# A fused attention and expert kernel: the long product with V behind the third exp scores, the laying of the maxima and block 0's product behind the sixth, the max units of a group in another order

## The chip, the cores and the metric

One core of one Trainium2 chip. The metric is the device time of one execution in microseconds (us); lower is better.

## What is computed

The input `x` is (2, 512, 128): two batches b of 512 tokens with 128 channels. The part that this change touches is causal attention with 16 heads of 8 channels: q, k and v come from modulated and rotated projections of `x`, and

```
scores = einsum('bhsd,bhtd->bhst', q, k) / sqrt(8)      # causal mask, softmax over t
out    = einsum('bhst,bhtd->bhsd', softmax(scores), v)
x      = x + out @ w_out.T
```

After it come a mixture of 2 shared and 8 routed experts, and a layer that applies the best 3 of 8 zones to each batch. All of it is float32 in the reference.

## The kernel before

**Tiling.** The 2 batches x 16 heads are taken as 8 groups n = 0 to 7 of 4 heads (`GROUPS`, `HG`). A softmax needs the row maxima ahead of the exp, so each group is scored twice. The *max scores* have queries on partitions: TensorE writes a *unit* (`scores_for_max`, L1407, and for the diagonal unit L1402) into one of three PSUM banks (`RING_BANKS`), and VectorE adds the mask and reduces it (`reduce_max`, L772). For groups 2 to 7 a group has 11 units, in this text P (two pieces of 256 columns, 2 of them), T (384 columns, 4 of them), F (512 columns, 4 of them) and D (block 0 of all four heads, 4 pieces of 128, one). Groups 0 and 1 have 12 of another cut. A unit can be written only when the unit three before it has been reduced (`wait_ring`).

**The maxima.** When all units of a group are reduced, GpSimd puts the maxima into a padded tile (`place_max`, L644 and L646), TensorE *lays* them (`lay_max_under_q`, L1420, 4 small matmuls into the unused bank of the sixth scores' slot), and ScalarE copies them under the queries (`copy_qm`, L1109).

**The exp scores.** They have keys on partitions, six products E0 to E5 per group (`scores_for_exp`: E0 to E3 at L1443, E4 at L1447, E5 at L1452) into two PSUM slots in turn: E(u) waits for the exp of E(u-2). E0 also waits for `copy_qm` of its group. ScalarE takes the exp of each (`exp`, L1105). GpSimd zeroes the triangles of a tile when two exps are done (`affine_select`, L672: c = 0, 1, 2) and, behind the last, spreads the last queries (L658), which the next E5 needs.

**The product with V.** `weigh_v` (L1467) has two parts: *block 0's product* `weigh_v(n, 0, 0, S)` (8 instructions, needs the triangle c = 0 and that the sums before are copied out) and the *long product*, key blocks 1 to 3 (24 instructions, needs all triangles). ScalarE copies the sums out of PSUM (`copy_pv`, L1115), and SyncE stores them.

**Order.** Everything is written out by hand. TensorE does a *pass* for each group n, and inside it interleaves E0 to E5 of group n, the long product of group n-1, the max units that `max_units(n, i)` hands out in 11 slices i (`maximum(i)`), the laying of group n+1 and block 0's product of group n. `LEAD` says how many units of group n+2 are done in pass n (7; `FIRST` is 4 for group 1). Before the change a pass from 2 to 5 is, for TensorE:

```
E0 F E1 F F | long product n-1 | D E2 E3 P P T E4 | block 0 of n | T | lay n+1 | T E5 T F
```

ScalarE's pass is exp 0, exp 1, `copy_pv(n-1)`, exp 2, a weight cast (`split_high`, L1200, where `SPLITS` has (n, 0)), exp 3, exp 4, `copy_qm(n+1)`, exp 5, a second cast (where it has (n, 2)). There are seven casts: (3,0) (3,2) (4,0) (4,2) (5,0) (5,2) (6,0). GpSimd's pass is triangle 0; wait for exp 3; `place_max(n+1)`; triangle 1; `split_low` (L618); wait for exp 5; triangle 2; spread last queries; `split_low`.

**SyncE's queue** goes in order. Its pass n issues for group n+3 `load_k` (L455), `pad_q` (L433, 4 transfers, waits until group n+1's units are written), `pad_k` (L446), `load_q` (L461), then `store_sums(n)` (L466, waits for `copy_pv(n)`) and the weight loads of `EXPERT_LOADS[n]` (L474, waited for by `split_high`). Around them stand `gather(0)` in pass 3 (L483 and L488, waits until the sums of groups 0 to 3 are stored) and in pass 4 `store_inverse(0)` (L496, waits for `invert(0)`, L791, which VectorE does behind unit 8 of group 6) and `spread_inverse(0)` (L504). The last weight load, k = 6, stands behind `store_sums(4)`.

Of the kernel before, what the change touches and what calls it, by code (L numbers as in the profile page):

```python
# [14 lines left out]
P = 128  # L15
B, S, D = 2, 512, 128
NT = B * S
H, HD = 16, 8
HG = 4
NG = H // HG  # L20
GROUPS = B * NG
# [12 lines left out]


SPREAD_UNITS = [[(j, qb, i * 2 * P) for i, qb in enumerate(blocks)] for blocks in ((0, 1), (2,), (3,)) for j in range(HG)]
PAIRED_UNITS = [[(2 * h2 + i, 1, i * 2 * P) for i in range(2)] for h2 in range(2)]
PAIRED_UNITS += [[(j, qb, 0)] for qb in (2, 3) for j in range(HG)] + [[(j, 0, j * P) for j in range(HG)]]
MX_UNITS = [SPREAD_UNITS if n < 2 else PAIRED_UNITS for n in range(GROUPS)]
MX_LIST = [(n, u) for n in range(GROUPS) for u in range(len(MX_UNITS[n]))]  # L40
RING_BANKS = (0, 1, 7)

# [9 lines left out]
N_UNITS = len(UNITS)  # L52


LEAD, FIRST = 7, 4
BY_PE = 1
SPILLS = 2
SLICES = 11
# [5 lines left out]
def units_to(n, u=0):  # L64

    return sum(len(x) for x in MX_UNITS[:n]) + u

# [6 lines left out]

RING_ORDER = [("max", 0, _u) for _u in range(len(MX_UNITS[0]))]
RING_ORDER += [("max", 1, _u) for _u in range(2)] + [("lay", 0)] + [("max", 1, _u) for _u in range(2, FIRST)]
# [70 lines left out]
def program(nc, io, scratch, out):  # L147
# [9 lines left out]
    with ctx:  # L157
# [255 lines left out]
        def _(sp):  # L413
# [12 lines left out]
            def pad_q(n):  # L426

                s = n % 2
                if n >= 2:
                    sp.wait_ge(mx_full, units_to(n - 1) if n < 4 else units_to(n - 1) - 1)  # L430
                for j in range(HG):
                    q = head_rows(j)
                    sp.dma_start(f32_of(q_pad[s][q, j, :]), laid(n, 0)[q, :]).then_inc(q_padded[s], 16)  # L433
# [157 lines left out]
        def _(pool):  # L591
# [72 lines left out]
            for n in range(GROUPS):  # L664
                for c in range(3):

                    pool.wait_ge(exp_done, STU * n + 2 * c + 2)
                    if c == 1 and n + 1 < GROUPS:
                        place_max(n + 1)
                    for o in ((0,) if c < 2 else (0, 2 * P)):  # L670
                        tri = probs[n % 2][:, c, :, o:o + P]
                        last = G.affine_select(out=tri, in_=tri, compare_op=ALU.is_ge, fill=0.0, base=0,  # L672
                                               pattern=[[0, HG], [1, P]], channel_multiplier=-1)
                    last.then_inc(masked, 1)
                    if c == 2 and n + 1 < GROUPS:
                        spread_last_queries(n + 1)
                    if n == 0 and c == 0:
                        turn(1)
                    if n == 0 and c == 1:
                        spread_last_queries(0)  # L680
                        turned(1)
                    if n == 0 and c:

                        pool.wait_ge(hi_ready, 4 + c)
                        pool.wait_ge(rep_ready, 2 * BY_PE + 2)
                        for written in spilled:
                            pool.wait_ge(written, 16 * SPILLS)
                        G.tensor_tensor(qk_lo[:, c - 1, :], roped[:, c - 1, :], f32_of(qk_hi[:, c - 1, :]),
                                        ALU.subtract).then_inc(lo_ready, 1)
                    if c and (n, 2 * c - 2) in SPLITS:  # L690
                        split_low(SPLITS[n, 2 * c - 2])
# [37 lines left out]
        def _(dve):  # L729
# [34 lines left out]
            def reduce_max(n, u):  # L764
# [3 lines left out]
                dve.wait_ge(mx_full, units_to(n, u + 1))  # L768
                for j, qb, o in MX_UNITS[n][u]:
                    width = P * (qb + 1)  # L770
# [252 lines left out]
        def _(act):  # L1023
# [63 lines left out]
            def exp(n, u):  # L1087
                s = n % 2
                c, h2 = divmod(u, 2)
                act.wait_ge(st_full, STU * n + u + 1)  # L1090
                if n >= 2 and u == 0:
                    act.wait_ge(pv_full, n - 1)
                if n == 1 and u == 4:
                    act.wait_ge(roped_ready, 6)
                at_ = slot_of("exp", n, u)
                if c < 2:
                    w = S - c * P
                    o, scores = probs[s][:, c, 2 * h2:2 * h2 + 2, 0:w], ST[:, at_:at_ + 2, 0:w]
                elif h2 == 0:
                    o = probs[s][:, 2, :, 0:2 * P]  # L1100
                    scores = ST[:, at_:at_ + 2, :].rearrange("p b (j q) -> p (b j) q", j=2)
                else:
                    o = probs[s][:, 2, :, 2 * P:3 * P]
                    scores = ST[:, at_, :].rearrange("p (j q) -> p j q", j=HG)
                A.activation(o, scores, ACT.Exp, scale=float(1.0 / np.sqrt(np.float32(HD)))).then_inc(exp_done, 1)  # L1105
# [5 lines left out]
            def copy_pv(n):  # L1111
                act.wait_ge(pv_full, n + 1)
                if n >= 2:
                    act.wait_ge(stored[n % 2], 16 * (n // 2))
                A.copy(o_sb[n % 2][:], PV).then_inc(pv_copied, 1)  # L1115
# [77 lines left out]
            def split_high(k):  # L1193

                hi, lo, c, at_ = chunks[k]
                act.wait_ge(ld_raw[k], 16)
                if k == UP_COLS // S:
                    for written in spilled:
                        act.wait_ge(written, 2 * 16 * SPILLS)
                A.copy(hi[:, c:c + S], raw[:, at_:at_ + S]).then_inc(w_hi, 1)  # L1200
# [25 lines left out]
            for n in range(GROUPS):  # L1226
                exp(n, 0)
                if n == 1:
                    take_hi(1)
                exp(n, 1)  # L1230
                if 0 < n < GROUPS - 1:
                    copy_pv(n - 1)
                exp(n, 2)
                if n == 0:
                    copy_v(1)
                if (n, 0) in SPLITS:
                    split_high(SPLITS[n, 0])
                exp(n, 3)
                exp(n, 4)
                if n == 0:  # L1240
                    take_hi(0)
                if n + 1 < GROUPS:
                    copy_qm(n + 1)
                if n == GROUPS - 1:
                    exp_of_minus_logits(0)
                exp(n, 5)
                if (n, 2) in SPLITS:
                    split_high(SPLITS[n, 2])
# [30 lines left out]
        def _(pe):  # L1279
# [103 lines left out]
            def scores_for_max(n, u):  # L1383
                s = n % 2
                pieces = MX_UNITS[n][u]
                if n == 0:
# [111 lines left out]
            def project_out(b):  # L1498
                pe.wait_ge(onorm_ready, b + 1)
                pe.wait_ge(ld_small, 16)  # L1500
                if b == 0:
                    wait_ring("out", 0)
                    T.matmul(ring("out", 0), small[:, W_OUT:W_OUT + D], packed_out[:],
                             start=True, stop=True).then_inc(proj_ready, 1)
                else:
                    pe.wait_ge(last_norm, 1)
                    T.matmul(MISC, small[0:EARLY, W_OUT:W_OUT + D], packed_out[0:EARLY, :], start=True, stop=False)
                    T.matmul(MISC, small[:, W_LAST:W_LAST + D], o_sb[1][:], start=False,
                             stop=True).then_inc(proj_ready, 1)
# [123 lines left out]
                T.matmul(MISC[:, 80:80 + TOPZ], ones_row[:], zw[:, b, :], start=True, stop=True).then_inc(z_bc, 1)  # L1633


            for n in range(GROUPS):

                def maximum(i):
                    for unit in max_units(n, i):
                        scores_for_max(*unit)  # L1640

                scores_for_exp(n, 0)
                maximum(0)
                scores_for_exp(n, 1)
                maximum(1)
                maximum(2)
                if n:
                    weigh_v(n - 1, 1, P, S)
                    weigh_v(n - 1, 2, 2 * P, S)
                    weigh_v(n - 1, 3, 3 * P, S)  # L1650
                maximum(3)
                scores_for_exp(n, 2)
                if n == GROUPS - 1:
                    project_out(0)
                scores_for_exp(n, 3)
                maximum(4)
                maximum(5)
                maximum(6)
                scores_for_exp(n, 4)
                if n == GROUPS - 1:  # L1660
                    route_experts(0)
                weigh_v(n, 0, 0, S)
                maximum(7)
                if n + 1 < GROUPS:
                    lay_max_under_q(n + 1)
                maximum(8)
                scores_for_exp(n, 5)
                maximum(9)
                maximum(10)
            up(0)  # L1670
            weigh_v(GROUPS - 1, 1, P, S)
            weigh_v(GROUPS - 1, 2, 2 * P, S)
# [107 lines left out]
```

## Time and profile before

| | us |
|---|---|
| median of 3 runs (lowest, highest) | 180.97 (180.79, 181.07) |
| the profiled execution, whole | 180.98 |
| its span, first to last instruction | 179.1 |
| attention passes 1 to 7 | from 34.0 to about 90 |

Times of rows are us from the span's start. In a row, "x24" is the number of instructions merged, and a bracket at the end is the idle time of the engine ahead of it and what ended it. PE is TensorE (PEld its weight loads), DVE VectorE, ACT ScalarE, POOL GpSimd, SPq SyncE's DMA queue. Matmuls are pipelined: the distance between two starts tells what one costs the engine, not its duration.

### The profile page before, as it was taken

The page shows a single profiled execution, that of the slowest core. Times are in us where ns is not written, and L with a number is a line of the kernel's source. Part 1 is how long each engine was busy: PE and PEld are TensorE (multiplying, and loading weights), DVE is VectorE, ACT ScalarE, POOL GpSimd, SP SyncE. Part 2 cuts the span into 40 slices and gives each one's busy share as a digit, 9 for nine tenths or more (in the row PEclk, how much of TensorE's full clock was granted, in tenths as well). Part 3 has the DMA queues.
Part 4 walks back from the last instruction along what each step waited for, and adds up shares of the span by engine and source line. Part 5 has one row for each costly group of instructions (what it writes and reads, how often), then busy time and mean ns, then how long its engine had stood idle before and what let it go on. Part 6 is the DMA issues. An engine that isn't in the chain of part 4 may idle for free.

```text
span 179.1 us, 3278 instructions
## 1 busy us (share of the span) xinstructions
PE 168.9 (94%) x943; PEld 116.8 (65%) x944; DVE 138.9 (78%) x444; ACT 134.3 (75%) x224; POOL 93.8 (52%) x117
## 2 busy tenths in 40 slices
PE   6899999899999999988999999996999989999992
PEld 2656575565666666653758767864687867788881
DVE  5588989989898899980586999699799658637551
ACT  3569177688768888889734787953879999999970
POOL 5508088985463969688532522021769931676000
PEclk9999999999999999999999999999999999999999
DMA  4824775676686567520110899960760000001001
GB/s 144 294 46 107 191 203 159 218 234 213 166 267 208 143 194 194 164 94 5 62 51 17 231 345 344 347 178 4 241 230 0 0 4 0 0 2 59 0 4 59
DMA packets 15349, 24.28 MB, mean 136 GB/s; under 512 B 2844, under 2 KB 4828, under 8 KB 15308
## 3 DMA queue, kind: packets, MB, share of 16 engines
q1 hardware_dynamic: 14532, 23.29, 42.2%
q10 hardware_dynamic: 800, 0.79, 1.7%
q8 instruction: 8, 0.13, 0.3%
q14 instruction: 9, 0.07, 0.1%
HBM read 18.71 MB, written 5.27 MB: 134 GB/s over the span
## 4 chain that ended last, share of the span: by engine, by line
PE 70%; DVE 11%; ACT 7%; issue 6%; POOL 4%; DVEq 0%; ACTq 0%; POOLq 0%
PE psum L1407 11%; PE psum L1540 10%; PE psum L1541 9%; PE psum L1542 9%; PE psum L1467 8%; PE psum L1443 7%; PE psum L1286 3%; PE psum L1338 2%; PE psum L1352 2%; ACT t_probs L1105 2%; DVE psum L772 2%; DVE t_raw L924 1%; PE psum L1402 1%; ACT t_q_pad L1155 1%; PE psum L1447 1%
## 5 line engine op out<-in xcount | busy, mean ns | idle before, releaser
L772 DVE CUSTOM_DVE_ANT_0 psum<-psum,t_causal 128x128 f32<-128x128 f32 (+3 forms) x128 | 58.6, 525 | 5.8 <-PE psum L1407 3.0
L1105 ACT ACTIVATE t_probs<-psum 128x1024 f32<-128x1024 f32 (+2 forms) x48 | 40.9, 883 | 8.2 <-PE psum L1443 5.2
L1407 PE MATMUL psum<-t_stacked,t_q_pad 96*128 96x256 f32 (+2 forms) x104 | 33.3, 391 | 0.5 <-DVE t_row_max L772 0.2
L1407 PEld LDWEIGHTS psum<-t_stacked,t_q_pad 96*128 96x128 f32 x104 | 18.4, 189 | 12.4 <-DVE t_row_max L772 10.2
L672 POOL TENSOR_SCALAR_AFFINE_SELECT t_probs<-t_probs 128x512 f32<-128x512 f32 x32 | 20.5, 651 | 9.0 <-ACT t_probs L1105 9.0
L944 DVE SCALAR_TENSOR_TENSOR t_q_pad<-psum,t_zw_all,t_q_pad 128x512 fp32r<-128x512 f32 x24 | 17.8, 748 | 9.3 <-ACT t_q_pad L1153 9.2
L1139 ACT ACTIVATE psum<-psum 128x512 f32<-128x512 f32 x40 | 23.4, 586 | 0.9 <-PE psum L1542 0.3
L703 POOL TENSOR_TENSOR t_q_pad<-t_raw,t_q_pad 128x512 fp32r<-128x512 f32 x8 | 10.8, 1357 | 21.0 <-ACT t_q_pad L1155 21.0
L1467 PE MATMUL psum<-t_probs,t_v_all 128*32 128x512 f32 (+3 forms) x256 | 20.6, 439 | 0.0
L772 DVE DVE_READ_ACCUMULATOR2_ANT t_row_max<- 128x1 f32 x128 | 18.0, 141 | 0.0
L1153 ACT ACTIVATE t_q_pad<-psum,t_zw_all 128x512 fp32r<-128x512 f32 x24 | 16.5, 688 | 1.2 <-PE psum L1542 0.6
L1443 PE MATMUL psum<-t_q_two,t_k_pad 104*128 104x512 f32 (+1 forms) x48 | 13.5, 380 | 0.4 <-ACT t_q_two L1109 0.4
L1540 PE MATMUL psum<-t_stacked,t_up_hi 128*128 128x512 f32 x32 | 13.8, 430 | 0.0
L1541 PE MATMUL psum<-t_stacked,t_up_lo 128*128 128x512 f32 x32 | 12.6, 394 | 0.0
L1542 PE MATMUL psum<-t_stacked,t_up_hi 128*128 128x512 f32 x32 | 12.6, 393 | 0.0
L947 DVE TENSOR_TENSOR t_q_pad<-psum,t_q_pad 128x512 fp32r<-128x512 f32 x16 | 10.9, 680 | 1.7 <-ACT t_q_pad L1155 1.3
L931 DVE TENSOR_TENSOR psum<-psum,t_stacked 128x512 f32<-128x512 f32 x16 | 11.0, 690 | 1.4 <-DVE t_top L852 0.7
L1467 PEld LDWEIGHTS psum<-t_probs,t_v_all 128*32 128x32 f32 x256 | 6.5, 109 | 7.8 <-issue 2.9
L1155 ACT CAST t_q_pad<-psum 128x512 fp32r<-128x512 f32 x16 | 9.4, 588 | 1.2 <-DVE psum L931 1.0
L1540 PE MATMUL psum<-t_q_pad,t_dn_hi 128*128 128x512 f32 x24 | 9.8, 408 | 0.4 <-POOL t_q_pad L703 0.2
L1443 PEld LDWEIGHTS psum<-t_q_two,t_k_pad 104*128 104x128 f32 x48 | 8.4, 189 | 2.5 <-issue 0.9
L1541 PE MATMUL psum<-t_q_pad,t_dn_lo 128*128 128x512 f32 x24 | 9.5, 396 | 0.0
(233 smaller groups left out, 369.6 us busy)
## 6 DMA issues: line engine op xcount, KB each, us to landing
t_stacked<-scratch SPq DMA_DIRECT2D x16, 256.0 KB, 5.7
t_probs<-in_L_ffn_Wa SPq DMA_DIRECT2D x2, 1024.0 KB, 11.5
scratch<-t_o_sb SPq DMA_DIRECT2D x7, 256.0 KB, 2.1
t_raw<-in_experts SPq DMA_DIRECT2D x7, 256.0 KB, 3.6
t_stacked<-scratch SPq DMA_DIRECT2D x9, 192.0 KB, 3.7
t_q_pad<-scratch SPq DMA_DIRECT2D x28, 48.0 KB
scratch<-t_dn_hi SPq DMA_DIRECT2D x2, 512.0 KB, 3.4
t_q_two<-scratch SPq DMA_DIRECT2D x5, 192.0 KB, 2.6
```

Of the source, the lines that this page charges most:

```text
L672: last = G.affine_select(out=tri, in_=tri, compare_op=ALU.is_ge, fill=0.0, base=0, pattern=[[0, HG], [1, P]], channel_multiplier=-1)
L772: last = V.tensor_tensor_reduce(scores, scores, causal[:, S - width:S], 1.0, 3 * BIG, ALU.add, ALU.max, row_max[s][:, qb, j:j + 1])
L944: V.scalar_tensor_tensor(h_lo[i % SLOTS], hidden_of(i), weight_of(i), f32_of(h_hi[i % SLOTS]), ALU.mult, ALU.subtract).then_inc(lo_done, 1)
L1105: A.activation(o, scores, ACT.Exp, scale=float(1.0 / np.sqrt(np.float32(HD)))).then_inc(exp_done, 1)
L1139: A.activation(o, pair_of(i)[:, 0, :], func, scale=scale).then_inc(act_done, 1)
L1153: A.activation(h_hi[i % SLOTS], hidden_of(i), ACT.Identity, scale=weight_of(i)).then_inc(hi_done, 1)
L1407: last = T.matmul(bank[:, o:o + width], q_pad[s][0:TOP, j, qb * P:(qb + 1) * P], stacked[0:TOP, n, 0:width], start=True, stop=True)
L1443: last = T.matmul(ST[:, at_ + i, 0:S - c * P], k, q[:, c * P:S], start=True, stop=True)
L1467: last = T.matmul(PV[32 * j:32 * j + 32, lo:hi], v_all[:, v0:v0 + 32], probs[n % 2][:, c, j, o:o + hi - lo], start=(kb == 0 and lo == 0), ...
L1540: T.matmul(o, hi, x_hi, start=start, stop=False)
L1541: T.matmul(o, lo, x_hi, start=False, stop=False)
L1542: return T.matmul(o, hi, x_lo, start=False, stop=stop)
```

## The change

TensorE's pass, `LEAD` and the order of a group's units change, with two calls that move on ScalarE and GpSimd. From 2 to 5, TensorE's pass is now

```
E0 T T E1 D T E2 F | long product n-1 | F E3 P E4 P F E5 | lay n+1 | F | block 0 of n | T
```

In passes 0 and 1 the units are those of the old order (pass 0: E0 T T E1 T T E2 F F F E3 F E4 P P E5, lay, T, block 0, T T). `LEAD` is 5, so that pass 0 does two units less and pass 6 two more. In pass 7, which has no units, the order stays. `pad_q` for groups 5 to 7 waits for one unit more, since the last unit of a group now reads the padded queries.

```diff
-PAIRED_UNITS = [[(2 * h2 + i, 1, i * 2 * P) for i in range(2)] for h2 in range(2)]
-PAIRED_UNITS += [[(j, qb, 0)] for qb in (2, 3) for j in range(HG)] + [[(j, 0, j * P) for j in range(HG)]]
-MX_UNITS = [SPREAD_UNITS if n < 2 else PAIRED_UNITS for n in range(GROUPS)]
+HEAD_PAIRS = [[(2 * h2 + i, 1, i * 2 * P) for i in range(2)] for h2 in range(2)]
+THREE, FOUR = [[[(j, qb, 0)] for j in range(HG)] for qb in (2, 3)]
+DIAGONAL = [[(j, 0, j * P) for j in range(HG)]]
+PAIRED_UNITS = HEAD_PAIRS + THREE + FOUR + DIAGONAL
+TURNED_UNITS = HEAD_PAIRS + FOUR[0:2] + THREE[0:3] + DIAGONAL + THREE[3:4] + FOUR[2:4]
+MX_UNITS = [SPREAD_UNITS if n < 2 else PAIRED_UNITS if n == 2 else TURNED_UNITS for n in range(GROUPS)]
...
-LEAD, FIRST = 7, 4
+LEAD, FIRST = 5, 4
...
-                    sp.wait_ge(mx_full, units_to(n - 1) if n < 4 else units_to(n - 1) - 1)
+                    sp.wait_ge(mx_full, units_to(n - 1) - (n == 4))
...
+                    if c == 1 and 2 <= n < GROUPS - 1:
+                        place_max(n + 1)
                     pool.wait_ge(exp_done, STU * n + 2 * c + 2)
-                    if c == 1 and n + 1 < GROUPS:
+                    if c == 1 and n < 2:
                         place_max(n + 1)
...
                 exp(n, 1)
-                if 0 < n < GROUPS - 1:
-                    copy_pv(n - 1)
                 exp(n, 2)
                 if n == 0:
                     copy_v(1)
                 if (n, 0) in SPLITS:
                     split_high(SPLITS[n, 0])
+                if 0 < n < GROUPS - 1:
+                    copy_pv(n - 1)
                 exp(n, 3)
...
+            for n in range(GROUPS - 1):
...
                 scores_for_exp(n, 0)
                 maximum(0)
-                scores_for_exp(n, 1)
                 maximum(1)
+                scores_for_exp(n, 1)
                 maximum(2)
+                maximum(3)
+                scores_for_exp(n, 2)
+                maximum(4)
                 if n:
                     weigh_v(n - 1, 1, P, S)
                     weigh_v(n - 1, 2, 2 * P, S)
                     weigh_v(n - 1, 3, 3 * P, S)
-                maximum(3)
-                scores_for_exp(n, 2)
...
+                maximum(5)
                 scores_for_exp(n, 3)
-                maximum(4)
-                maximum(5)
                 maximum(6)
                 scores_for_exp(n, 4)
...
-                weigh_v(n, 0, 0, S)
                 maximum(7)
-                if n + 1 < GROUPS:
-                    lay_max_under_q(n + 1)
                 maximum(8)
                 scores_for_exp(n, 5)
+                lay_max_under_q(n + 1)
                 maximum(9)
+                weigh_v(n, 0, 0, S)
                 maximum(10)
```

## Rows read from the trace of the kernel before

**Rows 1.** The page: busy time by engine

```profile
PE 168.9 (94%) x943; PEld 116.8 (65%) x944; DVE 138.9 (78%) x444; ACT 134.3 (75%) x224; POOL 93.8 (52%) x117
```

**Rows 2.** Stretches from E0 to E0, passes 0, 3, 6: busy PE, PEld, DVE, ACT, POOL; clock

```profile
24.57:34.04 9.47, 8.54 (x45) 5.23 (x43) 8.97 (x39) 6.83 (x12) 8.37 (x11) 1.00 0.59 174
...
50.52:58.75 8.23, 8.21 (x64) 5.27 (x64) 7.46 (x35) 6.66 (x10) 4.78 (x8) 1.00 0.75 227
...
75.21:83.03 7.82, 6.80 (x54) 3.69 (x53) 5.15 (x23) 6.90 (x11) 5.90 (x10) 1.00 0.28 94
```

**Rows 3.** The order of time, TensorE, pass 3 (E0 at 50.52)

```profile
50.52 0.63 PE L1443 MATMUL psum<-t_q_two,t_k_pad 104*128 104x512 f32 x2
...
51.68 0.67 PE L1407 MATMUL psum<-t_stacked,t_q_pad 96*128 96x512 f32 x2
52.29 1.50 PE L1467 MATMUL psum<-t_probs,t_v_all 128*32 128x384 f32 x24
53.72 0.50 PE L1402 MATMUL psum<-t_k_pad,t_q_two 96*128 96x512 f32 x1
54.06 0.87 PE L1443 MATMUL psum<-t_q_two,t_k_pad 104*128 104x384 f32 x4
54.77 1.09 PE L1407 MATMUL psum<-t_stacked,t_q_pad 96*128 96x256 f32 x5
55.70 0.63 PE L1447 MATMUL psum<-t_q_two,t_k_pad 104*128 104x256 f32 x4
56.26 1.06 PE L1467 MATMUL psum<-t_probs,t_v_all 128*32 128x512 f32 x8
57.25 0.44 PE L1407 MATMUL psum<-t_stacked,t_q_pad 96*128 96x384 f32 x1
57.53 0.40 PE L1420 MATMUL psum<-t_minus_ident_b,t_max_pad 128*128 128x128 bf16 x4
```

**Rows 4.** The order of time, VectorE, pass 3: around the two products

```profile
52.96 0.73 DVE L772 CUSTOM_DVE_ANT_0 psum<-psum,t_causal 128x512 f32<-128x512 f32 x1
53.61 0.14 DVE L772 DVE_READ_ACCUMULATOR2_ANT t_row_max<- 128x1 f32 x1
54.26 0.30 DVE L772 CUSTOM_DVE_ANT_0 psum<-psum,t_causal 128x128 f32<-128x128 f32 x1 [0.51 <-PE psum L1402]
...
57.73 0.57 DVE L772 CUSTOM_DVE_ANT_0 psum<-psum,t_causal 128x384 f32<-128x384 f32 x1 [0.26 <-PE psum L1407]
```

**Rows 5.** The order of time, end of pass 0 (E5 is L1452)

```profile
30.21 1.06 PE L1467 MATMUL psum<-t_probs,t_v_all 128*32 128x512 f32 x8
...
32.87 0.47 PE L1452 MATMUL psum<-t_stacked 104*128 104x512 f32 x1 [0.51 <-POOL t_stacked L658]
```

**Rows 6.** The order of time, ScalarE, passes 4 and 6

```profile
62.09 0.59 ACT L1115 COPY t_o_sb<-psum 128x512 f32<-128x512 f32 x1 [0.58 <-PE psum L1467]
...
80.01 0.61 ACT L1200 CAST t_dn_hi<-t_raw 128x512 fp32r<-128x512 f32 x1
80.52 1.73 ACT L1105 ACTIVATE t_probs<-psum 128x768 f32<-128x768 f32 x2
...
82.40 0.58 ACT L1109 CAST t_q_two<-psum 8x512 fp32r<-8x512 f32 x1 [0.15 <-PE psum L1420]
```

**Rows 7.** SyncE's queue, 62.7 to 74.4 us

```profile
62.70 0.34 SPq L466 DMA_DIRECT2D scratch<-t_o_sb  x1
...
70.40 0.42 SPq L496 DMA_DIRECT2D scratch<-t_sums  x1
...
73.95 0.43 SPq L474 DMA_DIRECT2D t_raw<-in_experts  x1
```

**Rows 8.** DMA issues of 73.9 to 74.5 us: count, KB, us to landing

```profile
t_raw<-in_experts SPq DMA_DIRECT2D x1, 256.0 KB, 4.4
```

**Rows 9.** TensorE: warm-up matmuls, and its longest silence later on

```profile
1.39 3.36 PE L1286 MATMUL psum<-t_warm 128*128 128x512 bf16 x8 [1.39 <-POOL t_warm L593]
...
122.64 0.28 PE L1614 MATMUL psum<-t_ident_r,t_gate 128*32 128x128 f32 x1 [1.62 <-DVE t_gate L878]
```

More of the change, by code:

```diff
@@ L1633, in zone_spread @@
                 T.matmul(MISC[:, 80:80 + TOPZ], ones_row[:], zw[:, b, :], start=True, stop=True).then_inc(z_bc, 1)
-            for n in range(GROUPS):
+            for n in range(GROUPS - 1):
                 def maximum(i):
@@ L1643, in _ @@
                 maximum(0)
+                maximum(1)
                 scores_for_exp(n, 1)
-                maximum(1)
                 maximum(2)
+                maximum(3)
+                scores_for_exp(n, 2)
+                maximum(4)
                 if n:
@@ L1650, in _ @@
                     weigh_v(n - 1, 3, 3 * P, S)
-                maximum(3)
-                scores_for_exp(n, 2)
-                if n == GROUPS - 1:
-                    project_out(0)
+                maximum(5)
                 scores_for_exp(n, 3)
-                maximum(4)
-                maximum(5)
                 maximum(6)
                 scores_for_exp(n, 4)
-                if n == GROUPS - 1:
-                    route_experts(0)
-                weigh_v(n, 0, 0, S)
                 maximum(7)
-                if n + 1 < GROUPS:
-                    lay_max_under_q(n + 1)
                 maximum(8)
                 scores_for_exp(n, 5)
+                lay_max_under_q(n + 1)
                 maximum(9)
+                weigh_v(n, 0, 0, S)
                 maximum(10)
+            last = GROUPS - 1
+            scores_for_exp(last, 0)
+            scores_for_exp(last, 1)
+            weigh_v(last - 1, 1, P, S)
+            weigh_v(last - 1, 2, 2 * P, S)
+            weigh_v(last - 1, 3, 3 * P, S)
+            scores_for_exp(last, 2)
+            project_out(0)
+            scores_for_exp(last, 3)
+            scores_for_exp(last, 4)
+            route_experts(0)
+            weigh_v(last, 0, 0, S)
+            scores_for_exp(last, 5)
             up(0)
```

## The prediction

> **What bounds the kernel now.** I read the page first: TensorE is busy 94%, VectorE 78% and ScalarE 75% [rows 1]. Busy time says little of a pipelined engine, so next the stretches from one E0 to the next. Pass 3 takes 8.23 us, and passes 1 to 5 are alike; in it VectorE is busy 7.46 us, ScalarE 6.66, and the granted clock is full, 2.4 GHz [rows 2]. No engine is full by itself. The order of time shows why: TensorE and VectorE take turns. During the long product TensorE writes no unit for 1.43 us (52.29 to 53.72), during block 0's product none for 0.99 us [rows 3], and VectorE, which has three banks in hand at most, runs dry behind both: 0.51 and 0.26 us [rows 4]. TensorE then waits for a bank elsewhere.
>
> How much can come back? TensorE's own cost of a pass is the sum of distances between starts: E0 or E1 0.47 us (51.68 is two of these and one F of 0.23 behind 50.52), E2 and E3 together 0.71, long product 1.43, E4 with the turn to the next product 0.56, block 0's product 0.99, and a T behind a product 0.28 (57.25 to 57.53) [rows 3]. With a plain T at 0.18, P at 0.23, E5 at 0.24 and the laying at 0.21 (estimates by columns from F), it comes to some 7.6 us. VectorE needs 7.46 less what it pays for running dry. So 0.6 us a pass is the ceiling, and TensorE sets it.
>
> **The change, part by part.** Each removes and adds no arithmetic; only places move.
>
> *A pass from 2 to 5.* I walk TensorE from E0 = 0: E0, T, T, E1, D to 1.53. The second T behind D needs the bank of the first T: written 0.47, read by VectorE 0.48 later (57.25 to 57.73 [rows 3, 4]), reduced some 0.63 after that with the read-out (F takes 0.65 + 0.14 from 52.96 to the end of 53.61's row, a T in proportion): 1.63, so 0.1 us of wait. T and E2 to 2.16, F to 2.39, the turn 0.1 and the long product 1.43: 3.92, call it 3.95. Then F 0.34 (the first matmul behind a product costs what D does, 53.72 to 54.06 [rows 3]), E3 0.35, P 0.23, E4 0.47, P 0.23, F 0.23, E5 0.24: the laying begins at 6.04; laying 0.21, F 0.23, turn and block 0's product 1.09, T 0.28: **7.85 us**, against 8.23. VectorE still runs dry at the long product, by about 0.35 us, but no longer at block 0's: F, F and the rest of a P are in hand, some 1.9 us for a hole of 1.7. That gap costs nothing as long as TensorE is the fuller engine.
>
> *Covers.* The laying waits for `place_max`: the last F is reduced at 3.95 + 0.54 + 0.79 = 5.28, placing and its signals are put at 0.65 more (an estimate: two small GpSimd operations, each between 0.2 and the 0.58 of the shortest ScalarE row [rows 6]): 5.93, just ahead of 6.04. `place_max` no longer waits for exp 3; that matters in pass 6, below, and in the others the laying was not late. ScalarE: the long product ends later, so `copy_pv` begins at 4.1 rather than 3.3, but behind exp 2 and the cast it no longer waits 0.58 us [rows 6]. Then exp 3, exp 4, `copy_qm` end at about 7.1; the next E0 wants it at 7.85. exp 5 now stands behind a later laying; triangle 2 has the time to the next long product, 4 us, to hide.
>
> *Pass 1* keeps the old order of units for group 2: D (some 1.05 us of VectorE, by its four pieces) is last, and `place_max(2)` waits for exp 3: the laying is 0.3 later. 8.15 us.
>
> *Pass 0.* E5 is started at 32.87 by GpSimd's spreading of the last queries (L658), whose chain the change does not touch [rows 5]. Block 0's product stood ahead of it at 30.21, in TensorE's idle time. Now the laying, T, block 0's product and two T come behind: 0.30 + 0.21 + 0.28 + 1.09 + 0.35, so E0 of pass 1 is at **35.1 instead of 34.04** [rows 2]: 1.06 us lost. The two units fewer of `LEAD` 5 give nothing here, since pass 0 waits for GpSimd; they are done in pass 6, where VectorE was busy 5.15 of 7.82 us [rows 2], beside other work.
>
> *Sum so far.* E0 of pass 4 = 35.1 + 8.15 + 2 x 7.85 = 58.95 (before: 58.75), of pass 5 66.8, of pass 6 some 74.65, with 0.2 for the padded queries of group 7, whose loads move later with the queue: 74.85 (before: 75.21). Pass 6, free of waits, would take 7.35, since its laying no longer waits for exp 3: E0 of pass 7 at 82.2 against 83.03.
>
> *SyncE's queue.* This is the cover that fails. `copy_pv(3)` began at 62.09 [rows 6], and its store went at 62.70 [rows 7]; now it begins at 58.95 + 4.1 = 63.05, **0.96 later**. Everything behind it is a chain: the gather waits until the store landed, then the loads of group 7, `store_inverse` at 70.40, its landing, `spread_inverse`, `store_sums(4)`, and the last weight load at 73.95 [rows 7], landed 4.4 us later [rows 8], at 78.35. `invert(0)` ends at 70.9, before the queue wants it at 71.4. So the load lands at 79.3. Its cast stood behind `copy_pv` at 80.01 [rows 6] and had 1.7 us to spare. Now it would begin at 74.85 + 3.35 = 78.2, ahead of `copy_pv(5)` and exp 3: ScalarE waits 1.1 us. From 79.35: cast 0.51, `copy_pv` 0.53, exp 3 and 4 1.73, `copy_qm` 0.58 [rows 6]: E0 of pass 7 at **82.75**, against 83.03.
>
> What follows (exps, triangle 2, route, gates, experts) hangs on that pass and moves with it. The sum is **0.28 us less**. The profiled execution took 180.98, which is the median of the runs within 0.01: 180.7. About 0.2%, 0.36 us, is what a measurement can tell from no change, so this counts as the same.
>
> *TensorE's clock.* Taking block 0's product out of pass 0 leaves TensorE silent from the end of its second P, about 30.2 by the same walk, to 32.87: 2.7 us. The longest silence of the trace behind its start is 1.62 us, and the clock stayed at 2.4 GHz; at the start eight matmuls of 512 columns took 3.36 us, 0.42 each, against F's 0.23 [rows 3, 9]. No row shows a gap of 2.7 us. If the clock fell to 1.2 GHz there and came back as it did at the start, some 3.4 us of matmuls would take twice their time: 1.6 us. The Trainium skill (TensorE: Matmul & The Clock Gate, What's actually happening) says that idleness brings the array back to 1.2 GHz, which speaks against this change. By it alone the sum would be a loss.
>
> **The rivals.**
> *A, faster:* the load does not bind, because pass 1 to 4 are shorter than I walk them or the transfers land sooner. Then E0 of pass 7 is at 82.2 or, with passes of 7.65, at 81.6: 180.15 to 179.6. For it: VectorE's need is below 7.46. Against: every pass has 0.1 us waits that I may have missed, not the reverse. Chance 0.26.
> *B, slower:* the pass stays above 8.0 us. Its place is the laying: TensorE reaches it 0.1 us behind the last placing, with block 0's product and E0 queued behind it, and E2 comes 0.1 us behind exp 0. If either is late by 0.2 us or more per pass, VectorE runs dry at block 0's product too. At 8.1 E0 of pass 6 is at 75.9 and of pass 7 at 83.3 to 83.5; at 8.23 the change brings only pass 0's loss and pass 6's gain, 84.0. That is 181.3 to 181.9. It decides from 8.0 on. Chance 0.26.
> *C, slower:* the clock falls in pass 0: 182.3. Chance 0.03.
> *D: the reorder does not do what it says*, VectorE's gaps only move, and the early loss and late gain cancel: 181.0. Its time is inside the forecast's range.
>
> **How the numbers follow.** The forecast, with D, has 0.45: E0 of pass 7 between 0.6 earlier and 0.4 later, 180.4 to 181.35; about 0.12 of it is beyond 0.2% faster. Faster 0.12 + 0.26 = 0.38; slower 0.26 + 0.03 and 0.01 of the forecast, 0.30; the same 0.32. The range reaches to A's middle and B's upper part: 179.8 to 181.8. The time is the likeliest case's.
>
> **What would show it.** Right: E0 to E0 at 7.8 to 7.9 us in passes 2 to 5; VectorE's idle behind block 0's product gone, one gap of about 0.35 us behind the long product; E0 of pass 1 at 35.1; the last weight cast (L1200) in pass 6 waiting for its DMA some 1 us, at 79.3. Wrong: passes of 8.0 or more, that cast without a wait, or a granted clock below full behind 32.87.

## The result, and the profile after

The changed kernel took 184.06 us (median of 4 runs, 182.80 to 185.32) against 181.02 (4 runs, 180.79 to 181.66): a ratio of 1.0151 by the measurement's own estimate (the two medians alone give 1.017), 95% interval 1.011 to 1.0192. It is slower; the forecast was 180.7, in a range up to 181.8. The execution that was profiled took 185.09, its span is 183.3. The four runs spread over 2.5 us, and their mean granted clocks were 0.971 to 0.989: the clock is in the result, and not by the same amount in each run.

The page of the kernel after, its slices of TensorE's work and clock (each 1/40 of the span, 4.58 us) and the chain:

```profile
PE 171.7 (94%) x944; PEld 118.0 (64%) x944; DVE 139.5 (76%) x444; ACT 134.7 (73%) x224; POOL 94.3 (51%) x117
...
PE   6999996799999999997999999996999989999993
...
PEclk9999999699999999997899999999999999999999
...
PE 67%; DVE 10%; ACT 7%; issue 6%; DMA 4%; SPq 2%; POOL 2%; DVEq 0%; ACTq 0%; POOLq 0%
```

The shares of busy time differ by two points at most [rows 1]. Two other things changed: the clock has two dips, and the chain that ended last now holds DMA (4%) and SyncE's queue (2%). In the kernel before it had neither:

```profile
PE 70%; DVE 11%; ACT 7%; issue 6%; POOL 4%; DVEq 0%; ACTq 0%; POOLq 0%
```

Next the stretches from E0 to E0, passes 0 to 6, but for 3 and 4 (busy PE, PEld, DVE, ACT, POOL; then clock, DMA share, GB/s):

```profile
24.98:37.00 12.02, 9.38 (x42) 5.26 (x41) 8.15 (x35) 6.95 (x12) 10.91 (x14) 0.87 0.61 188
...
37.00:45.40 8.40, 8.40 (x64) 5.28 (x63) 7.89 (x33) 6.65 (x9) 3.85 (x7) 0.98 0.66 217
45.40:53.36 7.96, 7.96 (x64) 5.13 (x63) 7.58 (x33) 6.15 (x8) 3.77 (x8) 1.00 0.48 148
...
69.22:77.57 8.35, 8.24 (x63) 5.01 (x63) 7.99 (x34) 7.27 (x11) 6.33 (x10) 1.00 0.52 140
77.57:86.63 9.06, 7.70 (x57) 4.11 (x56) 5.66 (x25) 6.92 (x10) 6.88 (x10) 0.91 0.33 114
```

Against [rows 2]: pass 0 takes 12.02 us, not 9.47; pass 2 takes 7.96 (3 and 4: 7.92 and 7.94), as meant; pass 5 takes 8.35 and pass 6 9.06 instead of 7.82. The middle of the attention got faster, and both of its ends much slower.

The end of pass 0, in order of time, answers to [rows 5]:

```profile
29.82 0.99 PE L1412 MATMUL psum<-t_stacked,t_q_pad 96*128 96x256 f32 x4
33.28 0.47 PE L1457 MATMUL psum<-t_stacked 104*128 104x512 f32 x1 [2.47 <-POOL t_stacked L661]
...
33.80 0.60 PE L1412 MATMUL psum<-t_stacked,t_q_pad 96*128 96x384 f32 x1
34.33 1.93 PE L1472 MATMUL psum<-t_probs,t_v_all 128*32 128x512 f32 x8
```

TensorE is silent for 2.47 us ahead of E5. Block 0's product behind it then takes 1.93 us, where it took 1.06. The same stretch, and one behind the second dip, as busy times and granted clock:

```profile
33.30:36.90 3.60, 3.60 (x16) 1.46 (x17) 0.62 (x2) 1.18 (x2) 3.60 (x5) 0.58 0.81 278
84.90:88.50 3.60, 3.60 (x14) 1.31 (x12) 0.00 (x0) 1.98 (x4) 3.33 (x4) 0.53 0.03 11
```

A mean of 0.58 and 0.53 is nearly all of it at 1.2 GHz. Ahead of the second dip stands the last weight cast of pass 6, with SyncE's queue and E5 of that pass, in order of time:

```profile
76.67 0.59 SPq L469 DMA_DIRECT2D scratch<-t_o_sb  x1
77.30 0.43 SPq L477 DMA_DIRECT2D t_raw<-in_experts  x1
...
82.35 0.62 ACT L1205 CAST t_dn_hi<-t_raw 128x512 fp32r<-128x512 f32 x1 [1.47 <-DMA t_raw<-in_experts]
82.88 0.58 ACT L1120 COPY t_o_sb<-psum 128x512 f32<-128x512 f32 x1
...
84.22 0.50 PE L1457 MATMUL psum<-t_stacked 104*128 104x512 f32 x1 [1.36 <-ACT t_probs L1110]
```

The load that was issued at 73.95 [rows 7] goes at 77.30; its cast waits 1.47 us, behind it the copy of sums and exp 3, and E5 waits 1.36 us for exp 3. Up to that silence TensorE was busy without a gap: its 7.70 of the 9.06 us of pass 6 are all but the 1.36.

### The profile page after: what moved, and what is told of

Its sections match the earlier page's. It is cut to its first block, busy times and chain, and to the rows that moved or that the text cites. A ratio compares the mean times of both kernels' runs of the same rounds, so it can differ in the third digit from the quotient of the medians.

```text
span 183.3 us, 3279 instructions
## 1 busy us (share of the span) xinstructions
PE 171.7 (94%) x944; PEld 118.0 (64%) x944; DVE 139.5 (76%) x444; ACT 134.7 (73%) x224; POOL 94.3 (51%) x117
## 4 chain that ended last, share of the span: by engine, by line
PE 67%; DVE 10%; ACT 7%; issue 6%; DMA 4%; SPq 2%; POOL 2%; DVEq 0%; ACTq 0%; POOLq 0%
PE psum L1545 10%; PE psum L1412 10%; PE psum L1546 9%; PE psum L1547 9%; PE psum L1472 8%; PE psum L1448 6%; PE psum L1291 4%; DMA t_raw<-in_experts 3%; ACT t_probs L1110 2%; PE psum L1343 2%; PE psum L1357 2%; DVE t_raw L929 1%; ACT t_q_pad L1160 1%; DMA scratch<-t_sums 1%; DVE t_raw L933 1%
## 5 line engine op out<-in xcount | busy, mean ns | idle before, releaser
L1110 ACT ACTIVATE t_probs<-psum 128x1024 f32<-128x1024 f32 (+2 forms) x48 | 40.3, 882 | 11.7 <-PE psum L1448 9.9
L1412 PE MATMUL psum<-t_stacked,t_q_pad 96*128 96x256 f32 (+2 forms) x104 | 34.9, 397 | 0.3
L1472 PE MATMUL psum<-t_probs,t_v_all 128*32 128x512 f32 (+3 forms) x256 | 22.2, 465 | 0.0
L1448 PE MATMUL psum<-t_q_two,t_k_pad 104*128 104x512 f32 (+1 forms) x48 | 15.3, 405 | 0.0
L1448 PEld LDWEIGHTS psum<-t_q_two,t_k_pad 104*128 104x128 f32 x48 | 9.2, 206 | 2.8 <-ACT t_q_two L1114 1.6
```

Source lines behind the costliest of these rows:

```text
L1412: last = T.matmul(bank[:, o:o + width], q_pad[s][0:TOP, j, qb * P:(qb + 1) * P], stacked[0:TOP, n, 0:width], start=True, stop=True)
L1448: last = T.matmul(ST[:, at_ + i, 0:S - c * P], k, q[:, c * P:S], start=True, stop=True)
L1472: last = T.matmul(PV[32 * j:32 * j + 32, lo:hi], v_all[:, v0:v0 + 32], probs[n % 2][:, c, j, o:o + hi - lo], start=(kb == 0 and lo == 0), ...
```

## The experiments

Twelve kernels beside the change. Medians and ratios are against runs of the kernel before on the same chip (181.3 to 181.4 there).

**1. Fill the silence.** The changed kernel, with

```diff
                 maximum(8)
+                if n == 0:
+                    pe.wait_ge(v_copied, KB * B)
+                    keep_warm(10, PV)
                 scores_for_exp(n, 5)
```

> The changed kernel with ten 512-column bf16 matmuls (some 2.2 us of TensorE) into the still unused sums bank between the second P and E5 of pass 0. Theory 1 (the 2.5 us of silence there drops the granted clock to 1.2 GHz, seen from 33.9 to 37.3 us of the changed kernel's trace): the clock stays at 2.4 GHz in pass 1, E0 of pass 1 comes at 35.5 instead of 37.0, and the whole is about 1.5 us shorter than the changed kernel, about 182.5, some 0.8% above the kernel before. Rival (the clock record is a by-product and the time is lost to the order, with block 0's product behind E5): E0 of pass 1 stays near 37.0 and the whole near 184.

182.0 us, ratio 1.0038 (1.001 to 1.0066). Eight of ten runs had a clock of 0.998 or more and took 181.5 to 182.4; the two at 0.991 took 183.94 and 183.97. The profiled one is of these two, and its fall begins in pass 6, behind a silence of 1.63 us (last row below). In it the silence of pass 0 is filled and the stretch behind E5 is at full clock:

```profile
30.56 2.33 PE L1291 MATMUL psum<-t_warm 128*128 128x512 bf16 x10
33.20 0.47 PE L1457 MATMUL psum<-t_stacked 104*128 104x512 f32 x1 [0.30 <-POOL t_stacked L661]
...
34.07 1.07 PE L1472 MATMUL psum<-t_probs,t_v_all 128*32 128x512 f32 x8
...
83.07 0.49 PE L1457 MATMUL psum<-t_stacked 104*128 104x512 f32 x1 [1.63 <-ACT t_probs L1110]
```

Pass 0 is 10.62 us instead of 12.02, E0 of pass 1 at 35.52. Adding work made the kernel 2.1 us faster. In the profiles 1.40 us of that lie in pass 0. The second fall, by the mean clock, came in two of these ten runs only.

**2. Silence alone, in the kernel before.** In pass 0 only, in effect:

```diff
-                weigh_v(n, 0, 0, S)
                 maximum(7)
+                scores_for_exp(n, 5)
+                weigh_v(n, 0, 0, S)
                 lay_max_under_q(n + 1)
                 maximum(8)
-                scores_for_exp(n, 5)
```

> The kernel before with one thing moved: in pass 0 block 0's product, the laying and the two units behind it come after E5, so TensorE is silent for some 2.5 us ahead of E5. Theory 1: the granted clock falls to 1.2 GHz soon after, and pass 0 ends 1.1 us later by the move and about 1.5 us by the clock: 183.0 to 183.6. Rival (silence is harmless, as 1.62 us were): only the move, about 182.0, clock 0.998.

186.24 us, ratio 1.0268 (1.0212 to 1.0323), clocks 0.972 to 0.991: the clock falls, as theory 1 said, and the time is 2.6 us beyond what it allowed. The silence is 2.32 us, and by the mean clocks of the two passes TensorE was at 1.2 GHz for about twice as long as in the changed kernel. Passes 0 and 1:

```profile
25.08:37.94 12.86, 10.05 (x45) 5.99 (x43) 9.24 (x39) 6.83 (x12) 10.45 (x13) 0.86 0.61 190
37.94:47.60 9.66, 9.65 (x63) 6.04 (x62) 7.45 (x33) 6.36 (x9) 4.17 (x7) 0.83 0.55 182
```

**3. The same order, silence filled** with `keep_warm(9, PV)` ahead of E5.

> e4_silence (the kernel before with pass 0's product, laying and two units behind E5) with nine warm-up matmuls in the silence. Theory (of e4_silence's 4.9 us the clock took all but the move): clock full, E0 of pass 1 about 1.1 to 1.6 us later than in the kernel before, the whole 182.5 to 183.0. Rival (the order costs them): above 184.5.

183.52 us, ratio 1.0112 (1.0086 to 1.0138), clock 1.0 in all four runs; 0.5 us more than the theory allowed:

```profile
24.90:36.81 11.91, 10.69 (x54) 6.04 (x53) 8.99 (x39) 6.83 (x12) 10.02 (x12) 1.00 0.60 191
36.81:45.05 8.24, 8.21 (x63) 5.29 (x63) 7.45 (x35) 6.33 (x9) 4.60 (x8) 1.00 0.68 223
```

Of 4.9 us lost in experiment 2, 2.7 are the clock (in the profiles 0.95 and 1.42 us in the two passes) and 2.2 the move. The move was put too low: 2.44 us in pass 0. Five T stand behind E5 here, against three in the kernel before and in the change, and the ring makes TensorE wait 0.37 us for VectorE among them.

**4. The last load earlier**, in SyncE's pass 3:

```diff
-EXPERT_LOADS = [(), (0, 1), (2, 3), (4, 5), (6,), (), (), ()]
+EXPERT_LOADS = [(), (0, 1), (2, 3), (4, 5, 6), (), (), (), ()]
```

> The changed kernel with the last weight load (k = 6) issued in SyncE's pass 3 with 4 and 5, instead of in pass 4 behind store_sums(4). Theory (the load binds pass 6): the cast of pass 6 no longer waits for its DMA (1.47 us before), pass 6 from E0 to E0 falls from 9.06 to about 7.4, the second fall of the clock (at 85.1 us) goes with the silence ahead of E5, and the whole is some 1.7 us or more below the changed kernel, about 182.3. Rival (something else sets pass 6, the placing or the copy of sums): pass 6 stays above 8.5 and the whole above 183.5.

183.83 us, ratio 1.0133 (1.0109 to 1.0157). Passes 5 and 6:

```profile
69.52:78.60 9.08, 8.23 (x63) 5.00 (x63) 7.97 (x34) 7.25 (x11) 6.32 (x10) 1.00 0.64 172
78.60:86.16 7.56, 7.10 (x57) 4.10 (x56) 5.67 (x25) 6.69 (x10) 6.13 (x9) 1.00 0.22 83
```

Pass 6 is what it should be, 7.56, and the second dip is gone, but pass 5 has grown by 0.73, and the whole stays 1.5 us above the 182.3 expected. The rival is right on the whole (above 183.5) and wrong on pass 6.

**5. Both**, experiments 1 and 4.

> Both: filler in pass 0 and the early load. If the two costs are separate they add: clock full throughout, about 3.2 us below the changed kernel, 180.7, near the kernel before (181.0). What is left is then pass 0's moved product (1.06 us lost) against 0.3 us won in each of passes 2 to 5 and 0.5 in pass 6. If they are one cost (the early fall only shifts what the load would have hidden) it stays near 182.3.

181.86 us, ratio 1.0022 (1.0005 to 1.0039), clock 0.997 or more in all ten runs. Not the 180.7 expected: pass 5 takes 9.22. Its first P, in order of time:

```profile
73.74 0.51 PE L1412 MATMUL psum<-t_stacked,t_q_pad 96*128 96x256 f32 x2 [0.99 <-DMA t_q_pad<-scratch]
```

The load now stands ahead of group 7's padded queries in SyncE's queue, and TensorE waits for those.

**6. Loads earlier still**, with the filler: `EXPERT_LOADS = [(), (0, 1, 2), (3, 4, 5, 6), (), ...]`.

> The changed kernel with the filler of e1_filler, and the weight loads issued earlier: k = 2 in SyncE's pass 1, k = 3 to 6 in pass 2, none in passes 3 and 4, so that nothing stands ahead of the gather and of group 7's padded queries. Theory (SyncE's queue sets passes 5 and 6: in e3_both the first P of pass 5 waited 0.99 us for the padded queries): pass 5 takes 7.95 instead of 9.2, pass 6 7.55, E0 of pass 7 is at 83.5, the whole 1.2 us below e3_both, about 180.8. Rival (pass 5 is long for another reason, invert(0) or the order of units): pass 5 stays near 8.3 or above, and the whole at 181.5 or more.

A miss: 183.15 us (181.99 to 186.21), ratio 1.0085 (1.0046 to 1.0125), worse than 5. Three of the seven runs had a clock of 0.981 or 0.991 and took 184.5 us or more. The profiled one had a full clock. The same wait has moved one pass forward, to group 6's padded queries, and doubled:

```profile
66.35 0.51 PE L1412 MATMUL psum<-t_stacked,t_q_pad 96*128 96x256 f32 x2 [1.89 <-DMA t_q_pad<-scratch]
```

Pass 4 takes 10.11 us; passes 5 and 6 are free, 7.96 and 7.55. TensorE's 1.89 us of silence here had no fall of the clock behind it.

**7. These loads in the kernel before.**

> The kernel before with only the early loads of e5_loads. Its casts never waited (the last was 1.7 us behind its landing), so the theory says no change, within 0.2%. Rival (the loads' place in the queue is worth something by itself, and e7_both's gain is theirs): about 1 us below the kernel before.

181.83 us, ratio 1.0017 (0.9996 to 1.0039): not told from no change by the runs, and not a gain; so the loads are no hidden gain of experiment 9. One of the twelve runs fell to a clock of 0.99 and took 185.2 us. The trace shows a cost: pass 4 takes 9.08 us instead of 8.24, by the same wait:

```profile
PE psum L1407 <- DMA t_q_pad<-scratch: 0.9, 1, 0.9
```

**8. Pass 0 put back.** The changed kernel, with

```diff
                 maximum(8)
-                scores_for_exp(n, 5)
-                lay_max_under_q(n + 1)
-                maximum(9)
-                weigh_v(n, 0, 0, S)
+                if n == 0:
+                    weigh_v(n, 0, 0, S)
+                    lay_max_under_q(n + 1)
+                    maximum(9)
+                    scores_for_exp(n, 5)
+                else:
+                    scores_for_exp(n, 5)
+                    lay_max_under_q(n + 1)
+                    maximum(9)
+                    weigh_v(n, 0, 0, S)
                 maximum(10)
```

> The changed kernel with pass 0 alone put back (block 0's product, the laying and one T ahead of E5, no filler, the loads as in the change). Theory: no silence, clock full at 34 us, E0 of pass 1 at 34.5; passes 2 to 5 at 7.95; the last weight load still late, so that pass 6 takes about 8.7 and the clock may fall once at 83: E0 of pass 7 about 83.5, the whole 181.0 to 182.5 by whether it falls. Rival (the order of the later passes costs something by itself): 183 or more.

179.97 us, ratio 0.9916 (0.989 to 0.9942): with the product and the laying ahead of E5 again in pass 0, the change is a gain, and a larger one than the 181.0 to 182.5 expected. Four of five runs had a full clock and took 179.8 to 180.0. The fifth, the profiled one, took 182.4 at 0.991. In it the last cast waited longer than ever, TensorE was silent for 2.36 us ahead of E5 of pass 6, and the clock fell behind it:

```profile
ACT t_dn_hi L1205 <- DMA t_raw<-in_experts: 2.4, 1, 2.4
```

The four runs at full clock were not profiled, so how long their cast waited is not known.

**9. Pass 0 put back, and the loads of experiment 6.**

> Pass 0 put back and the early loads of e5_loads: both costs of the change taken away. Theory: E0 of pass 7 at 34.5 + 8.4 + 4 x 7.95 + 7.55 = 82.3 against 83.4 of the kernel before at the same start, clock full: about 1.0 us below the kernel before. Rival (the new order of the passes brings nothing): the same as before or above.

180.83 us, ratio 0.9959 (0.9939 to 0.9979): half of the gain expected, and less than in 8. The profile shows the waits of 6, but small: TensorE waits twice for padded queries, 0.7 us in all, and pass 3 takes 8.29 us, pass 5 8.16. The profiled execution, at 180.03 us, is among the fastest of the twelve (180.0 to 184.89; two of them at clocks of 0.991 and 0.981), so the cause of the rest is argued and not shown.

**10. Pass 0 put back, the last load between the two deadlines**: behind group 7's loads and ahead of `store_inverse(0)`.

```diff
-EXPERT_LOADS = [(), (0, 1), (2, 3), (4, 5), (6,), (), (), ()]
+EXPERT_LOADS = [(), (0, 1), (2, 3), (4, 5), (), (), (), ()]
...
                     if n == NG:
+                        load_experts(6)
                         store_inverse(0)
```

> e6_pass0 (the change with pass 0 put back) with the last weight load (k = 6) issued in SyncE's pass 4 ahead of store_inverse(0): behind group 7's padded queries, which e3_both and e5_loads made late, and some 3 us earlier than in the change. Theory (each place in SyncE's queue has one deadline: the padded queries first, then the load): pass 4 and 5 at 7.95 to 8.1, pass 6 at 7.55 without a wait at the cast, no fall of the clock, E0 of pass 7 at 81.5 to 81.8 when pass 1 begins at 33.5: about 1.5 us below e6_pass0's 180.0 if that one waited 2.4 us in every run, 0.5 if not: 178.5 to 179.5. Rival (late sums or the padded queries bind again): 180 or more.

**179.50 us** (179.41 to 179.98), ratio 0.9901 (0.9881 to 0.9921), clock 0.998 or more in all six runs, at the upper edge of the forecast. It is the fastest kernel of the study, 1.8 us below the kernel before. Its passes 0 to 3, 5 and 6, and the last cast, which waits for nothing:

```profile
24.92:33.89 8.97, 7.89 (x43) 4.83 (x41) 8.04 (x34) 6.51 (x12) 7.87 (x10) 1.00 0.53 155
33.89:42.37 8.48, 8.48 (x63) 5.08 (x63) 7.95 (x33) 7.10 (x10) 6.91 (x11) 1.00 0.85 291
42.37:50.33 7.96, 7.96 (x63) 5.14 (x63) 7.59 (x33) 6.15 (x8) 3.78 (x8) 1.00 0.61 181
50.33:58.27 7.94, 7.94 (x63) 5.11 (x63) 7.55 (x33) 6.78 (x10) 5.13 (x9) 1.00 0.67 191
66.24:74.30 8.06, 8.06 (x64) 5.01 (x63) 7.97 (x34) 7.25 (x11) 6.33 (x10) 1.00 0.59 170
74.30:81.85 7.55, 7.10 (x56) 4.09 (x55) 5.67 (x25) 6.68 (x10) 6.14 (x9) 1.00 0.32 106
...
77.48 0.63 ACT L1206 CAST t_dn_hi<-t_raw 128x512 fp32r<-128x512 f32 x1
```

**11. The filler, and this load**: the change's own pass 0 with both indirect costs away.

> The changed kernel with the filler of e1_filler and the load of e9_mid: both indirect costs gone, pass 0 in the change's order. Theory: the moved product alone, 1.06 us, against e9_mid. Pass 6 at 7.55, pass 5 at 7.95 to 8.4 by the padded queries. Rival (the move costs more or less than its term): a difference outside 0.7 to 1.5 us.

181.31 us, ratio 0.9995 (0.9979 to 1.0011), clock 0.998 or more in all ten. Against experiment 10 the order of pass 0 alone costs 1.8 us, more than the 0.7 to 1.5 allowed: pass 0 takes 10.62 us here and 8.97 there, and the latter is 0.5 below the kernel before. E5 starts 8.30 us behind E0 in all three traces; to the next E0 it is then 2.32 us here, 1.17 in the kernel before with three T, and 0.67 in experiment 10 with two. Experiments 8 to 10 so do not put pass 0 back quite as it was: the third T now stands ahead of E5.

**12. The copy of sums put back** ahead of exp 2, in experiment 10's kernel.

```diff
                 exp(n, 1)
+                if 0 < n < GROUPS - 1:
+                    copy_pv(n - 1)
                 exp(n, 2)
...
-                if 0 < n < GROUPS - 1:
-                    copy_pv(n - 1)
                 exp(n, 3)
```

> e9_mid with copy_pv put back ahead of exp 2 on ScalarE, as in the kernel before. Theory (the move of copy_pv is needed since the long product now ends 4 us into the pass, after exp 1): ScalarE waits for the sums with exp 2 and the cast behind it, passes 2 to 5 grow to 8.2 to 8.5, and the whole is 1 to 3 us above e9_mid. Rival (ScalarE has slack enough): within 0.3 us of e9_mid.

184.17 us, ratio 1.0173 (1.0132 to 1.0214): 4.7 us above experiment 10, where 1 to 3 were expected. One of the four runs, at a clock of 0.991, took 185.6; the others 183.8 to 184.2. Passes 3 to 5 take 8.9 us. ScalarE's row of pass 3:

```profile
55.47 0.59 ACT L1121 COPY t_o_sb<-psum 128x512 f32<-128x512 f32 x1 [1.49 <-PE psum L1473]
```

It waits 1.49 us for the sums, with exp 2, exp 3 and exp 4 behind it. The move of `copy_pv` is what makes the later long product affordable.

## Why the prediction was wrong

By its own steps:

- **A pass from 2 to 5: right in kind, 0.1 us short.** 7.85 forecast, 7.92 to 7.96 measured in passes 2 to 4 (8.23 before). VectorE's idle behind block 0's product is gone, and behind the long product there is one gap of 0.36 us, 0.35 forecast. In this row of the kernel after it stands:

```profile
49.89 0.70 DVE L777 CUSTOM_DVE_ANT_0 psum<-psum,t_causal 128x512 f32<-128x512 f32 x1 [0.36 <-PE psum L1412]
```

- **Pass 1: 8.15 forecast, 8.48 measured** at full clock (experiments 5, 10 and 11, within 0.01). The walk took the old order of group 2 into account, but not what it does to the mix: by the program, pass 1 now has six F and two T, where passes 2 to 5, and pass 1 before, have four of each. VectorE is busy 7.95 us in it, against 7.59 in pass 2 and 7.46 in pass 1 before. No run took this mix away, so that it costs the 0.3 us is argued.
- **Pass 0, the move: right.** 1.06 us forecast; with a full clock pass 0 takes 10.62 against 9.47, 1.15. The remark beside it, that two units fewer give nothing while pass 0 waits for GpSimd, holds up to E5. What it leaves out is that a T taken from behind E5 does give time: experiment 10's pass 0 is 0.5 us shorter than before. No run separates the place of that T from `LEAD`.
- **TensorE's clock: the step that failed.** I found the silence (2.7 us; it was 2.47), had the row of a 1.62 us silence without a fall, worked out the price, 1.6 us, and then gave it a chance of 0.03 and left it out of the sum. The clock fell in all four runs of the change, by their mean clocks, and the fall in pass 0 cost 1.40 us (12.02 against 10.62). It was below 0.992 in all twelve runs of the three kernels with an unfilled silence there (the change, experiments 2 and 4), and never below 0.997 in the 62 runs of the kernel before beside the experiments. With nothing in the trace between 1.62 and 2.7 us, the row bounded neither side, and 0.03 was not read off anything. By the rule that the Trainium skill gives (TensorE: Matmul & The Clock Gate, What's actually happening), idleness brings back 1.2 GHz; the trace of the changed kernel agrees, 0.58 of full clock behind the silence. The price had weaker ground than it looks: the granted clock that the profile gives for the warm-up matmuls at the start is 1.00, and only their 0.42 us each spoke for half speed; the 3.4 us came out all the same, from 33.9 to 37.3. I had weighed the fall as a rival, at about the right price for pass 0 and the wrong chance.
- **SyncE's queue: right in mechanism, and larger.** The cast waited 1.47 us, 1.1 forecast. The whole queue was late by pass 0's loss (the last load goes 3.35 us later than before, 0.96 forecast, and takes 5.0 us to land, not 4.4), so its price rose with the first mistake. What I had not seen is that behind TensorE's silence there, 1.36 us, the clock falls a second time; in experiment 4, where the cast does not wait and the silence is 0.44 us, the profile has no second dip. Group 7's padded queries, put at 0.2 us, made pass 5 0.4 longer than passes 3 and 4.
- **The sum.** 3.0 us slower. In the profile E0 of pass 7 is at 86.63, 3.88 us behind the 82.75 of the walk: 0.41 by which attention starts later, 1.49 in pass 0 (nearly all the clock), 0.25 in pass 1, 0.27 in passes 2 to 4, 0.30 in pass 5 and 1.16 in pass 6; some 0.5 more follow behind it, where the clock is low until 88.4. Taking things away one by one: the filler gives 2.1 (184.06 to 182.0), the load's place 0.7 (to 181.3), pass 0's order 1.8 (to 179.5). What is left is the gain of the other passes together with the 0.5 us in pass 0, 1.8 us under the kernel before. The kernel before measured 181.0 to 181.4 beside these runs, so the parts are good to some 0.4 us.

Rival A, a pass shorter than walked, fell. So did B: passes 2 to 4 stayed below 8.0, and pass 5 came above it by its padded queries, not at the laying. C is what happened, but its 182.3 held only the one fall and the load's wait as forecast; the measured 184.06 lies above it by what the first loss did further on, the later queue and the second fall.

## What to carry to other kernels

A stretch in which TensorE waits is also a place where work is kept for free: move the work out and you pay for it twice, once for the move and once for the clock if it falls behind the silence. A shorter silence elsewhere that left the clock alone is no proof that this one will; ten matmuls that fill it, with no other use, are the test. In a queue that goes in order, each load has two neighbours with deadlines; when everything ahead is late by 1 us, look for the transfer with the least to spare, and place it between the deadlines rather than as early as possible.

## What the runs showed of the hardware

Silences of TensorE in the profiled executions, and what the granted clock did behind them. No fall: 1.59 to 1.62 us at one place behind attention, in all fourteen traces, and 1.89 us in pass 4 of experiment 6. A fall to 1.2 GHz: 2.47 us (the change, experiment 4) and 2.32 us (experiment 2) in pass 0; 1.36 us (the change), 1.63 us (experiment 1) and 2.36 us (experiment 8) ahead of E5 in pass 6. Each of these falls came 0.6 to 1.2 us behind TensorE's first matmul again. Length alone does not tell it, then: 1.89 us was harmless and 1.36 us was not, and TensorE was busy without a gap ahead of that one too. What separates them these traces do not show.

Nor does the program tell it. By the mean clocks, experiment 1 fell in 2 of 10 runs, 6 in 3 of 7, 8 in 1 of 5, 9 in 2 of 12, 12 in 1 of 4, and 7, which is the kernel before but for its loads, in 1 of 12; where a kernel fell once (0.990 or 0.991), that run was some 1.5 to 3.4 us slower than the median of its others. The changed kernel's four runs, 182.8 to 185.3 us, go with clocks of 0.989 to 0.971 in the same way, as far as four runs tell.
